# Attention stage: q normalised from one of two alternating banks, the logit scale folded into the squared norms, the layer-norm statistics copied by ScalarE

## What is computed

```python
h = einsum('bhid,oi,od->bho', x, weighted_sum, weight)      # image tokens
h = concatenate([h, txt], axis=1)
# attention: 16 heads of 16, over the 8 sequences of one position
a = layernorm(h)
q, k, v = split(a @ in_proj_weight.T + in_proj_bias)
ls = exp(minimum(logit_scale, log(100)))
attn = softmax(einsum('nhld,nhmd->nhlm', l2norm(q), l2norm(k)) * ls)
h = h + ((attn @ v) * head_scale) @ out_w.T + out_b
# a feed-forward layer: head-wise attention inside a token, a gate, 8 experts
h = h + ffn(layernorm(h))
```

## Time and profile before

| | |
|---|---|
| median of 3 runs | 916.53 us (912.55 to 917.62) |
| the profiled execution | 916.73 us, of which the span is 914.9 us |
| PE, PE weight loads | 808.9 us (88%), 517.0 us (57%) busy |
| DVE | 787.8 us (86%) busy |
| ACT, POOL | 321.7 us (35%), 398.9 us (44%) busy |
| instructions | 48,709 |

### The profile page before, as it was taken

How to read it: one execution, slowest core, us unless ns; L and a number is a source line. 1 busy time by engine, 2 the same in 40 slices (tenths; PEclk the granted TensorE clock), 3 DMA queues, 4 the chain that set the end, 5 groups by cost and what they waited for, 6 DMA issues and landing times.

```text
span 914.9 us, 48709 instructions
## 1 busy us (share of the span) xinstructions
PE 808.9 (88%) x20422; PEld 517.0 (57%) x20422; DVE 787.8 (86%) x1847; ACT 321.7 (35%) x797; POOL 398.9 (44%) x1122
## 2 busy tenths in 40 slices
PE   4999788888888888776999999999999999999997
PEld 3888455555555555444555555555555555555553
DVE  5898479999999999856789999999999999999996
ACT  4576334444444444212222322332233223322321
POOL 1421255555555555644334444434443344434111
PEclk9999989999999999857899999999999999999999
DMA  9973000000000000000000000000000000000000
GB/s 324 312 239 110 2 3 4 0 0 0 0 0 0 0 0 1 4 2 4 9 10 13 12 11 6 11 11 11 6 11 11 11 6 11 11 6 11 12 16 17
DMA packets 16692, 28.14 MB, mean 31 GB/s; under 512 B 3425, under 2 KB 11953, under 8 KB 16632
## 3 DMA queue, kind: packets, MB, share of 16 engines
q1 hardware_dynamic: 16632, 27.28, 9.0%
HBM read 22.44 MB, written 4.83 MB: 30 GB/s over the span
## 4 chain that ended last, share of the span: by engine, by line
DVE 27%; PE 15%; issue 10%; ACT 3%; DVEq 1%; POOL 1%; ACTq 0%; POOLq 0%
PE bank L589 6%; DVE acc L742 5%; DVE fq_t L778 3%; DVE h L789 3%; DVE smax L754 3%; DVE sc L757 3%; DVE pr_t L767 2%; DVE of L793 2%; PE bank L176 2%; DVE kv_t L780 2%; PE bank L177 2%; PE bank L178 1%; DVE x L774 1%; PE bank L616 1%; DVE h_t_l L798 1%
## 5 line engine op out<-in xcount | busy, mean ns | idle before, releaser
L833 POOL TENSOR_TENSOR qpad<-qraw,bq_s 128x256 f32<-128x256 f32 x37 | 26.8, 725 | 200.7 <-ACT qraw L682 200.7
L176 PE MATMUL bank<-we_h,h_t_h 128*128 128x512 f16 x296 | 113.8, 384 | 0.0
L177 PE MATMUL bank<-we_l,h_t_h 128*128 128x512 f16 x296 | 112.7, 381 | 0.0
L178 PE MATMUL bank<-we_h,h_t_l 128*128 128x512 f16 x296 | 112.5, 380 | 0.0
L742 DVE SCALAR_TENSOR_TENSOR acc<-bank,gate,acc 128x256 f32<-128x256 f32 x222 | 105.1, 474 | 5.1 <-PE bank L178 1.1
L176 PE MATMUL bank<-tokw_h,x_t_h 128*128 128x256 f16 x256 | 70.7, 276 | 12.2 <-DVE x_t_l L371 12.2
L177 PE MATMUL bank<-tokw_l,x_t_h 128*128 128x256 f16 x256 | 70.6, 276 | 0.0
L178 PE MATMUL bank<-tokw_h,x_t_l 128*128 128x256 f16 x256 | 70.5, 276 | 0.0
L600 PEld LDWEIGHTS bank<-pr_t,v 32*32 32x32 f32 x4736 | 48.0, 106 | 33.0 <-issue 33.0
L1076 POOL TENSOR_TENSOR rt<-rn 128x32 f32<-128x32 f32 x111 | 26.7, 240 | 84.7 <-DVE rn L1048 78.9
L946 ACT ACTIVATE pr<-sc 128x512 f32<-128x512 f32 x37 | 23.3, 630 | 108.0 <-DVE sc L992 108.0
(11 more groups left out here) (204 smaller groups left out, 2275.5 us busy)
## 6 DMA issues: line engine op xcount, KB each, us to landing
xbuf<-in_x SPq DMA_DIRECT2D x32, 512.0 KB, 4.6
out<-res SPq DMA_DIRECT2D x36, 128.0 KB
we_s<-in_we SPq DMA_DIRECT2D x4, 512.0 KB, 5.6
inw<-in_in_w SPq DMA_DIRECT2D x1, 768.0 KB, 11.4
wrep<-in_w_rep SPq DMA_DIRECT2D x1, 512.0 KB, 5.4
h_all<-in_txt SPq DMA_DIRECT2D x1, 512.0 KB
wst<-in_wst_in SPq DMA_DIRECT2D x1, 256.0 KB, 2.8
outw<-in_out_w SPq DMA_DIRECT2D x1, 256.0 KB, 10.6
```

What stands on the lines that cost most here:

```text
L176: nc.tensor.matmul(dst, a_h(c), b_h(c), start=start and c == 0, stop=False)
L177: nc.tensor.matmul(dst, a_h(c), b_l(c), start=False, stop=False)
L178: last = nc.tensor.matmul(dst, a_l(c), b_h(c), start=False, stop=stop and c == chunks - 1)
```

## The change

It has five parts.
1. `qn` reads q from the product's bank, unscaled, in place of a copy in SBUF. So that the bank may be held longer, the product goes to bank 1 and bank 7 in turn (`b_qk[p % 2]`). PE's wait before it is now for `a_qk` of two tiles before. ACT copies only k (`kr`, 256 columns in place of 512), and waits for `p_kpad`.
2. The logit scale goes into the squared norms. `inv_ls` is exp(-2 min(logit, log 100)); `half_ls` holds 0.5 WS² exp(-2 ...) for the q heads and 0.5 for the k heads; half of the sums of squares is now `max(ss, 1e-24) * half_ls`, so that `rn` comes out of the Newton steps with `ls` and 1/WS in it. The multiplication of `rn` by `ls` (before L1015) is gone.
3. The copy of `mv` into `cf_all` goes from DVE to ACT, behind the exponential; DVE's `bn_aggr` waits for the copy of the tile before (`a_keep`).
4. Two buffers in turn beside three make the loop body six tiles long on PE, ACT and DVE. POOL keeps three. The loop now covers tiles 6 to 29 in four turns, and tiles 0 to 5 and 30 to 36 are written out.
5. Three small operations are added on DVE before the stage's first tile.

```diff
--- before.py
+++ after.py
@@ -110,6 +110,8 @@
         wg_h, wg_l = halves("wg", [P, KC, E])
         we_h, we_l = halves("we", [P, KC, E, D])
         ls = sb("ls", [P, H])
+        inv_ls = sb("inv_ls", [P, H])
+        half_ls = sb("half_ls", [P, 2 * H])
         bd_s = sb("bd_s", [LAT, 1])
         bv_h, bv_l = halves("bv", [P, KC, P])
         bvec = sb("bvec", [P, D])
@@ -421,7 +423,7 @@
                         if k < 2:
                             linked(nc.vector.tensor_tensor(bias_l[k + 1][:, :], bias_l[k][:, :], bias_p[k][:, :], ALU.subtract))
 
-                    nc.vector.tensor_scalar(ls[:, :], ls[:, :], 4.605170185988091, None, ALU.min).then_inc(ls_min, 1)
+                    nc.vector.tensor_scalar(ls[:, :], ls[:, :], 4.605170185988091, -20.0, ALU.min, ALU.max).then_inc(ls_min, 1)
 
                 weight(0)
                 weight(1)
@@ -477,7 +479,7 @@
         shifted = sb("shifted", [P, 2 * H])
         rn = sb("rn", [P, 2 * H])
         rt = sb("rt", [P, 2 * H])
-        qkr = [sb(f"qkr{p}", [P, 2 * D]) for p in range(3)]
+        kr = [sb(f"kr{p}", [P, D]) for p in range(3)]
         qn = sb("qn", [P, H, HD])
         q_t = sb("q_t", [P, 8, 32])
         k_t = sb("k_t", [P, 8, 64])
@@ -519,14 +521,14 @@
...
-        b_xt, b_qk, b_v, b_s, b_o, b_ot, b_out = bank[0:7]
+        b_xt, b_qk, b_v, b_s, b_o, b_ot, b_out = bank[0], (bank[1], bank[7]), *bank[2:7]
...
@@ -907,8 +909,8 @@
                     sums(i, p, 1)
                     if real(i, 2):
                         pe.wait_ge(a_xtl, i + 3)
-                        wait(pe, a_qkr, i + 2)
-                        rows_times(b_qk[:, :], xt_h, xt_l, lambda c: inw_h[:, c, 0:2 * D],
+                        wait(pe, a_qk, i + 1)
+                        rows_times(b_qk[p % 2][:, :], xt_h, xt_l, lambda c: inw_h[:, c, 0:2 * D],
                                    lambda c: inw_l[:, c, 0:2 * D], slice(0, 2 * D)).then_inc(a_qkm, 1)
                     if real(i, 2):
                         wait(pe, a_v, i + 2)
@@ -926,11 +928,11 @@
                 rows_times(b_out[:, 0:D], bv_h, bv_l, lambda c: outw_h[:, c, :], lambda c: outw_l[:, c, :],
                            slice(3 * D, 4 * D)).then_inc(bvec_ps, 1)
                 head = ffn_pe(pe)
-                tiles_in_order(pe, body, 2, 3, 3, then=lambda i: in_tail(head, i))
+                tiles_in_order(pe, body, 2, 3, 6, then=lambda i: in_tail(head, i))
 
             @block.scalar
             def _(act):
-                nc.scalar.activation(ls[:, :], ls[:, :], ACT.Exp).then_inc(ls_ready, 1)
+                nc.scalar.activation(inv_ls[:, :], ls[:, :], ACT.Exp, scale=-2.0).then_inc(ls_ready, 1)
 
                 def body(i, p):
                     if real(i, 3):
@@ -944,12 +946,16 @@
                         act.wait_ge(a_sub, i + 1)
                         wait(act, a_prt, i)
                         nc.scalar.activation(pr[:, :, :], sc[:, :, :], ACT.Exp).then_inc(a_exp, 1)
+                    if real(i, -2):
+                        settle(act, tokw_ready)
+                        act.wait_ge(a_mv, i - 1)
+                        nc.scalar.activation(cf_all[:, bass.ds(i - 2, 1), 0:2].squeeze(1), mv[:, :], ACT.Copy).then_inc(a_keep, 1)
                     if real(i, 2):
                         act.wait_ge(a_qkm, i + 3)
                         wait(act, a_ss, i + 2)
-                        nc.scalar.activation(sq[:, :, :], b_qk[:, :], ACT.Square, scale=1.0 / WS).then_inc(a_sq, 1)
-                        wait(act, a_qk, i)
-                        nc.scalar.activation(qkr[(p + 2) % 3][:, :], b_qk[:, :], ACT.Copy, scale=1.0 / WS).then_inc(a_qkr, 1)
+                        nc.scalar.activation(sq[:, :, :], b_qk[p % 2][:, :], ACT.Square, scale=1.0 / WS).then_inc(a_sq, 1)
+                        wait(act, p_kpad, i)
+                        nc.scalar.activation(kr[(p + 2) % 3][:, :], b_qk[p % 2][:, D:2 * D], ACT.Copy, scale=1.0 / WS).then_inc(a_qkr, 1)
                     if real(i, 3):
                         act.wait_ge(a_xnps, i + 4)
                         wait(act, a_vm, i + 3)
@@ -964,13 +970,17 @@
                         nc.scalar.activation(vaug[(p + 2) % 3][:, :, 0:HD], b_v[:, 0:D], ACT.Copy, scale=1.0 / WS).then_inc(a_v, 1)
 
                 head = ffn_act(act)
-                tiles_in_order(act, body, 2, 3, 3, then=lambda i: in_tail(head, i))
+                tiles_in_order(act, body, 2, 3, 6, then=lambda i: in_tail(head, i))
 
             @block.vector
             def _(dve):
                 s3 = b_s[:, :].rearrange("p (h m) -> p h m", h=H)
                 o3 = b_o[:, 0:H * 17].rearrange("p (h d) -> p h d", d=17)
 
+                nc.vector.memset(half_ls[:, H:2 * H], 0.5)
+                dve.wait_ge(ls_ready, 1)
+                nc.vector.tensor_scalar(half_ls[:, 0:H], inv_ls[:, :], 0.5 * WS * WS, None, ALU.mult).then_inc(half_ready, 1)
+                dve.wait_ge(half_ready, 1)
                 dve.wait_ge(bvec_ps, 1)
                 nc.vector.tensor_scalar(bvec[:, :], b_out[:, 0:D], 1.0 / WS, None, ALU.mult).then_inc(bvec_ready, 1)
 
@@ -997,29 +1007,19 @@
                         nc.vector.bn_stats(st[:, :], hi).then_inc(a_st, 1)
                         settle(dve, tokw_ready)
                         dve.wait_ge(a_st, i - 1)
+                        wait(dve, a_keep, i - 2)
                         nc.vector.bn_aggr(mv[:, :], st[:, :]).then_inc(a_mv, 1)
                     if real(i, 0):
                         dve.wait_ge(a_exp, i + 1)
 
-                        nc.vector.transpose(pr_t[p][:, :, :], pr[:, :, :]).then_inc(a_prt, 1)
-                    if real(i, -2):
-
-                        settle(dve, tokw_ready)
-                        dve.wait_ge(a_mv, i - 1)
-                        nc.vector.tensor_copy(cf_all[:, bass.ds(i - 2, 1), 0:2].squeeze(1), mv[:, :]).then_inc(a_keep, 1)
-                    if real(i, 1):
-                        dve.wait_ge(p_rn, i + 2)
-                        if isinstance(i, int) and i == -1:
-                            dve.wait_ge(ls_ready, 1)
-
-                        nc.vector.tensor_tensor(rn[:, 0:H], rn[:, 0:H], ls[:, :], ALU.mult).then_inc(a_lsq, 1)
+                        nc.vector.transpose(pr_t[p % 3][:, :, :], pr[:, :, :]).then_inc(a_prt, 1)
                     if real(i, -1):
                         dve.wait_ge(a_av, i)
                         nc.vector.reciprocal(rsum[:, :], o3[:, :, HD:HD + 1]).then_inc(a_rsum, 1)
                     if real(i, 1):
                         dve.wait_ge(a_qkr, i + 2)
-                        dve.wait_ge(a_lsq, i + 2)
-                        nc.vector.tensor_tensor(qn[:, :, :], qkr[(p + 1) % 3][:, 0:D].rearrange("p (h d) -> p h d", d=HD),
+                        dve.wait_ge(p_rn, i + 2)
+                        nc.vector.tensor_tensor(qn[:, :, :], b_qk[(p + 1) % 2][:, 0:D].rearrange("p (h d) -> p h d", d=HD),
                                                 rn[:, 0:H].unsqueeze(2).to_broadcast([P, H, HD]),
                                                 ALU.mult).then_inc(a_qk, 1)
                     if real(i, -1):
@@ -1039,7 +1039,8 @@
 
 
                         dve.wait_ge(a_ss, i + 3)
-                        nc.vector.tensor_scalar(half_ss[:, :], ss[:, :], 1e-24, 0.5, ALU.max, ALU.mult).then_inc(a_half, 1)
+                        nc.vector.scalar_tensor_tensor(out=half_ss[:, :], in0=ss[:, :], scalar=1e-24, in1=half_ls[:, :],
+                                                       op0=ALU.max, op1=ALU.mult).then_inc(a_half, 1)
                         dve.wait_ge(a_half, i + 3)
                         nc.vector.tensor_scalar(shifted[:, :].bitcast(U32), half_ss[:, :].bitcast(U32), 1, None,
                                                 ALU.logical_shift_right).then_inc(a_shift, 1)
@@ -1056,7 +1057,7 @@
                         nc.vector.tensor_tensor(xt_l[:, :, :], b_xt[:, 0:D], xt_h[:, :, :], ALU.subtract).then_inc(a_xtl, 1)
 
                 head = ffn_dve(dve)
-                tiles_in_order(dve, body, 2, 3, 3, then=lambda i: in_tail(head, i))
+                tiles_in_order(dve, body, 2, 3, 6, then=lambda i: in_tail(head, i))
 
             @block.gpsimd
             def _(pool):
@@ -1075,12 +1076,12 @@
                                     pool.wait_ge(p_newton, n + 4 * k + m)
                                 step = nc.gpsimd.tensor_tensor(o[:, :], a[:, :], b[:, :], op)
                                 step.then_inc(p_newton if (k, m) != (2, 3) else p_rn, 1)
-                        raw = qkr[(p + 2) % 3]
+                        raw = kr[(p + 2) % 3]
                         settle(pool, consts_ready)
                         pool.wait_ge(a_qkr, i + 3)
                         pool.wait_ge(p_rn, i + 3)
                         wait(pool, a_qkt, i + 2)
-                        nc.gpsimd.tensor_tensor(kpad[:, :, 0:4:3, :], raw[:, D:2 * D].rearrange("p (a s d) -> p a s d", s=2, d=HD),
```

(11 more changed lines are left out.)

## The result

The changed kernel took 922.70 us (median of 8 runs, 919.61 to 930.61), the one before 914.68 us (8 runs, 912.36 to 917.62). The ratio is **1.0103, 95% interval 1.0067 to 1.0139**: slower, as forecast (922).

A forecast was written before the change was run, and what follows sets the result against it. DVE was taken to set the attention stage's pace, with PE 0.93 us per tile to spare. From 916.7 us, -22.4 + 8.7 + 1.2 + 8.4 + 5.1 + 4.8 = +5.8 gave 922 us, range 896 to 933.

The forecast's parts named there:

- the likeliest case: PE's six-tile attention loop is fetched anew in every turn: 922 us, between 914 and 931, chance 0.40.
- DVE's slots: DVE's time per attention tile: 0.69 us saved, 0.67 after POOL's Newton steps, a tile of 6.89 us.
- copy and multiplication 0.29, `qn` 0.40 by its form: DVE per tile: dropping both operations saves 0.29 us; `qn`, reading a bank as `on` does, falls from 0.74 to 0.34.
- The gain's total: DVE's saving over the attention stage: 0.67 us per tile, 33.4 tiles' worth, -22.4 us.
- Fetched anew: PE's six-tile loop, 10.2 instruction blocks, is not held on the chip but loaded every turn; some 93 packets against 45.
- Stalls inside the body: PE's waits for instruction blocks within the loop: 0.4 us per tile over 24 tiles, less 0.9 of before, +8.7 us.
- The jumps: PE's three jumps back to the loop's start: 2.8 us each for the target's missing block, +8.4 us, before further costs.
- the forecast's two cases: Second block at each PE jump: 3.4 us if asked for only then, 0 if both come together; half taken, +5.1.
- the clock's: Granted clock of 0.5 behind PE's three jumps: +4.8 us in the sum.
- The held loop: Rival: PE's six-tile loop stays on the chip and is silent from tile 12 on; 897 us, chance 0.15.
- the cheap jump: Rival: PE's loop is fetched anew, but both blocks at the jump come together and the clock stays up; 913 us, chance 0.22.
- The long `qn`: Rival: DVE's `qn` gets no shorter from the bank, so only 0.27 us per tile is saved; 932 us, chance 0.08.

The follow-up runs named there:

- The fast kernels: Variants whose loops are three tiles long, such as the change with three q and k banks (897.88 us) or the kernel before with only the scale folded (897.82 us).
- the shifted loop: The change with the bias product before the stage made five times, so PE's six-tile loop begins elsewhere in its instruction block: 923.18 us, ratio 1.0076.

## Why the prediction was right, point by point

**The time and the sign.** 922 was forecast and 922.7 measured, and the likeliest case is the one that came. That the sum comes out so close is partly luck: its terms' errors cancel, and the kernel before measured 914.7 in these runs where the forecast started from 916.7, so that the difference is 8.0 us and not 5.8. The terms below are read from the profiled execution, which is 13.9 us longer than that of the kernel before.

**DVE's slots: the tile was right to 1%, the reason was half wrong.** Forecast 6.89 us, measured 6.96. The step that failed is "copy and multiplication 0.29, `qn` 0.40 by its form". The pace is a circle: from the guess `rn` over twelve Newton operations on POOL to `qn`, and from `qn` over DVE's list to the next guess. Before, the way from `qn` to the next guess took from 217.69 to 220.82, as this row of the kernel before shows:

```profile
220.82 0.18 DVE L1048 TENSOR_SCALAR rn<-shifted 128x32 int32<-128x32 int32 x1
```

That is 3.13 us, and the rest of a tile of 7.56 is 4.43 from the guess to `qn`. With the scale folded alone they are 2.74 (from `qn` at 230.20 to the guess at 232.94 us) and 4.23 (232.94 to 237.17), 6.97 together. The multiplication stood between the guess and `qn` for 0.20 us, and the blocked `qn` lay on the way from `qn` to the guess for 0.39: that is all of the 0.59 between 7.56 and 6.97. The copy lay in DVE's time to spare ahead of the Newton steps' end and was worth nothing. The forecast saw that POOL "takes part of it back" and put it at 0.02; it took back the copy's whole slot.

**The gain's total.** Forecast -22.4. The fast kernels came out 17 to 19 us below the one before: 0.60 in place of 0.67 per tile, over 33 tiles, is 19.8.

**Fetched anew, not held: right.** 97 packets (93 forecast), 4 GB/s through the loop, against 45 and nothing with three tiles. The two gaps at the jump lie where counting put them: the second after 46 instructions, 43 forecast. The ground of that choice did not carry it, though: that blocks come one at a time and just ahead of use does not show how many are kept. They come so in the kernel before too, at 137.4 and 141.4 us, and its loop is kept.

**Stalls inside the body: too large.** Forecast 9.6 us over 24 tiles. In the profiled execution the 18 tiles not next to a jump are 4.5 us above 6.96 each together, 0.25 per tile: 2.6 in the first turn, 0.3, 1.0 and 0.6 in the others. The step that was mis-sized is 0.4 us per tile, which took two stalls in three tiles for typical. Where a boundary falls decides, as the shifted loop showed.

**The jumps: too small.** Forecast 8.4 + 5.1 + 4.8 = 18.3, measured 26.1. The second block is asked for only after the first, the upper of the forecast's two cases, but its gap is 2.1 to 2.4 us and not 3.4: 6.7 in three, between the half that was taken (5.1) and the whole (10.2). Nor is 3.9 us the least for a block: the two packets at the three jumps start 3.26, 3.39 and 3.05 us apart (from 202.77, 253.46 and 305.35 us). The sign "a gap before `L891` of 3 to 7 us" did not come: the gaps there are 1.89, 0.42 and 2.33 us. The term that was clearly too small is the clock's, the 4.8 of the sum, an estimate of 1.6 at each jump. No run shows that term by itself. What the changed kernel's trace shows in its place is a second tile behind each jump that has no gap of PE and takes 9.24, 9.29 and 9.25 us, 2.3 above 6.96, at a mean granted clock of 0.74, 0.73 and 0.73; the low clock (0.50 from 208 to 218 us) covers part of the first tile too. The last boundary inside the body, 1.37, 1.35 and 0.69 us of gap, is counted here and not under the stalls. How the rest divides between these the runs don't show.

**The range of the likeliest case.** 914 does not follow from the bounds given: with 0.3 us per tile, no second block and the clock up, the sum is -22.4 + 6.3 + 1.2 + 8.4 = -6.5, which is 910. The measured time lies far from that end.

**The rivals.** The held loop was wrong, the cheap jump too. The long `qn` was wrong for the bank, and its opposite was missed: that `qn` would be short without the bank.

**Not tried.** A second buffer for `rn` and `half_ss`, so that the guess for the next tile need not wait for `qn`, might open the circle; no run shows it.

## What to carry to other kernels

Before buffers are added, work out the period of all the counts that take turns: two banks beside three buffers doubled a loop that no one had meant to lengthen, and PE's loop alone cost 25 to 26 us. When an engine's gap says that it waited for no semaphore, count the packets of the instruction queue and look for traffic inside a loop: the loops of three tiles had none here, those of six 4 to 5 GB/s. And when one change bundles several edits, run each alone: here a single line held the whole gain, since it decided which of `qn` and `kpad` started first.

## What the runs showed of the hardware

- PE's instructions come in blocks of 256: the stalls without a semaphore lie 512 instructions apart in the kernel before (140.17 to 148.93 us), and 512, 767, 513 and 1,280 in the changed one. A packet has 16.4 KB, and in the changed kernel PE went on 2.15 to 2.90 us after the start of the last one before.
- PE's loop of three tiles, 1,318 instruction records a turn or 5.1 blocks, is kept (45 packets), one of six, 2,633 or 10.3 blocks, is fetched in each turn (97), and one of four, 1,739 to 1,777 or 6.9 blocks, in every second turn (78). A jump to a block that isn't there cost 8.4 to 9.1 us, the next block, the low clock and a gap of 0.7 to 1.4 us ahead of the jump included, when its target was 46 instructions before a block's end, and 4.1 to 6.5 when it was at a block's beginning. Why the loop of four tiles is fetched in only every second turn the runs don't show.
- DVE's `qn` with two inputs in SBUF and POOL's `kpad` hold each other up, and the one that starts second is long: `qn` 0.82 in place of 0.43, or `kpad` 0.78 in place of 0.62. With one input in a bank `qn` stays at 0.43, and `kpad` at 0.62, in either order. The one that starts first keeps its 0.62 or 0.42 us. The delays, 0.39 and 0.16 us, are shorter than what was left of the other operation (0.54 and 0.30).
